# Four reorderings in a two-layer graph-attention kernel: a PSUM copy changes engine, two casts, the score product and a transpose change place

## What is computed

```python
q, k, v = heads(x @ Wq + bq), heads(x @ Wk + bk), heads(x @ Wv + bv)       # 6 heads of 64
probs = softmax(q @ k.T / 8 + where(adj, 0, -9e15))
x = layernorm(x + concat(probs @ v) @ Wf + bf)
h = einsum('bnd,ade->bane', x, W); th = tanh(h)                              # 12 heads of 32
attn = leaky_relu(th @ w_src + (th @ w_dst).T, 0.2); attn = where(adj, attn, -999)
f = elu(softmax(attn) @ h + b); gate = sigmoid(x @ H_w.T + H_b)
x = layernorm(x + gate * f + (1 - gate) * x)
```

## Time and profile before

| | before |
|---|---|
| median of 3 runs | 1189.36 us (1188.29 to 1189.74) |
| the profiled execution, its own time | 1188.84 us |
| its span in the profile | 1187.0 us |
| TensorE busy | 1109.9 us, 94% |
| VectorE busy | 954.3 us, 80% |
| ScalarE busy | 945.2 us, 80% |
| GpSimd busy | 543.9 us, 46% |
| mean granted TensorE clock | 0.988 of full speed |

### The profile page before, as it was taken

The page is one execution under the profiler, slowest core; times in us unless marked ns, Lnnn a source line. Parts: engine busy times, 40 slices in busy tenths (PEclk is TensorE's granted clock), DMA queues, the critical chain, the costliest instruction groups (busy, mean ns, idle before and its releaser), DMA issues.

```text
span 1187.0 us, 25718 instructions
## 1 busy us (share of the span) xinstructions
PE 1109.9 (94%) x8428; PEld 902.9 (76%) x8428; DVE 954.3 (80%) x1958; ACT 945.2 (80%) x3447; POOL 543.9 (46%) x717
## 2 busy tenths in 40 slices
PE   6889999999999999999999999999999999997873
PEld 5667887878787787878778788877878877786652
DVE  5457888888888888888888887888888788888875
ACT  3248888888888888888888888888888888878875
POOL 0454544364454435445444544544454454444332
PEclk9899999999999999999999999999999999999997
DMA  9101001020100101010010101002010100100000
GB/s 257 54 2 54 15 25 57 8 68 15 61 15 18 65 8 68 15 60 15 15 63 12 68 15 61 15 8 68 14 68 15 62 15 8 41 15 15 15 14 21
DMA packets 25894, 44.67 MB, mean 38 GB/s; under 512 B 2462, under 2 KB 23714, under 8 KB 25762
## 3 DMA queue, kind: packets, MB, share of 16 engines
q1 hardware_dynamic: 23234, 41.91, 10.4%
q10 hardware_dynamic: 2496, 1.12, 0.5%
q0 software_dynamic: 32, 0.00, 0.0%
HBM read 30.43 MB, written 12.58 MB: 36 GB/s over the span
## 4 chain that ended last, share of the span: by engine, by line
PE 59%; ACT 23%; issue 8%; POOL 5%; DVE 3%; DMA 1%; ACTq 0%; POOLq 0%; DVEq 0%
ACT z L588 15%; PE ps_b L255 15%; PE ps_a L255 12%; PE ps_d L255 9%; PE ps_s L364 4%; ACT p1T L598 3%; PE ps_s L356 3%; PE ps_c L474 3%; POOL xT_lo L921 3%; PE ps_d L464 3%; PE ps_d L452 3%; PE ps_d L448 3%; PE ps_c L482 2%; ACT gate L664 2%; PE ps_b L411 1%
## 5 line engine op out<-in xcount | busy, mean ns | idle before, releaser
L588 ACT ACTIVATE z<-z,s 128x128 f32<-128x128 f32 x768 | 298.8, 402 | 0.5 <-DVE s L798 0.5
L958 POOL TENSOR_SCALAR s<-s 128x1 f32<-128x1 f32 x128 | 28.6, 224 | 311.8 <-DVE s L892 287.2
L973 POOL TENSOR_TENSOR p<-p,s 128x768 f32<-128x768 f32 x64 | 94.3, 1473 | 147.3 <-DVE s L804 147.3
L615 ACT ACTIVATE p<-ps_s,s 128x128 f32<-128x128 f32 x384 | 135.5, 372 | 29.4 <-DVE s L776 29.0
L588 ACT ACTIVATION_READ_ACCUMULATOR z<-z,s 128x1 f32 x768 | 154.4, 201 | 0.0
L464 PE MATMUL ps_d<-ident,z 128*128 128x128 f32 x768 | 120.0, 279 | 18.4 <-ACT z L588 8.9
L908 DVE SCALAR_TENSOR_TENSOR z<-ps_d,z 128x512 f32<-128x512 f32 x192 | 119.2, 676 | 6.3 <-ACT z L685 6.3
L981 POOL TENSOR_TENSOR thw<-th,w_sd 128x768 f32<-128x768 f32 x64 | 117.7, 1839 | 8.7 <-ACT th L636 8.5
L464 PEld LDWEIGHTS ps_d<-ident,z 128*128 128x128 f32 x768 | 90.7, 141 | 33.0 <-ACT gate L664 18.2
L598 ACT ACTIVATE p1T<-ps_d 128x512 f32<-128x512 f32 x192 | 113.4, 591 | 0.7 <-PE ps_d L464 0.7
L921 POOL TENSOR_TENSOR xT_lo<-x_cols,xT_hi 128x768 fp32r<-128x768 f32 x30 | 54.0, 1821 | 112.8 <-ACT xT_hi L555 112.8
(11 more groups left out here) (157 smaller groups left out, 3536.1 us busy)
## 6 DMA issues: line engine op xcount, KB each, us to landing
x_cols<-in_xT_dram SPq DMA_DIRECT2D x16, 768.0 KB, 6.4
xb<-in_x_dram SPq DMA_DIRECT2D x16, 768.0 KB, 4.9
out_dram<-y SPq DMA_DIRECT2D x64, 192.0 KB, 1.8
z<-in_L_gnn_Wq_dram SPq DMA_DIRECT2D x1, 576.0 KB, 6.3
p1T<-in_L_gnn_Wk_dram SPq DMA_DIRECT2D x1, 576.0 KB, 8.2
qT<-in_L_gnn_Wv_dram SPq DMA_DIRECT2D x1, 576.0 KB, 10.6
kT<-in_L_gnn_Wf_dram SPq DMA_DIRECT2D x1, 576.0 KB, 12.8
z<-in_L_gnn_W_dram SPq DMA_DIRECT2D x1, 576.0 KB, 11.6
```

The lines of the kernel that those rows point to most:

```text
L588: done = act.activation(z[:, a, :], z[:, a, :], ACT.Exp, bias=neg1[:, a:a + 1], accum_out=sum1[:, a:a + 1])
L615: last = act.activation(p0[:, o, i, :], ps_s[:, o, i * N:(i + 1) * N], ACT.Exp, bias=neg0[:, k:k + 1], accum_out=sum0[:, k:k + 1])
L973: pool.tensor_tensor(p0[:].rearrange("p o i n -> p (o i) n"), p0[:].rearrange("p o i n -> p (o i) n"), inv0.unsqueeze(2).broadcast_to([P, ...
```

## The change

It touches three engines' orders. TensorE: the mask and the scores of batch ta+1 are issued right behind `context` of batch ta (before: the mask behind `logits`, the scores at the head of the next turn), and `turn_f` stands behind `fill_a`. VectorE: the maximum of the scores of ta+1 stands behind `cols_R`; the reciprocal and scaling of f stand behind the second maxima; the first copy of p1T is made here, between the split and `cols_R`. ScalarE: that copy is gone, and the two casts of x in j = 3 stand behind the first and behind the second copy of v.

```diff
 # TensorE
-                        scores(g, 1 - par, j)
-                    if has_tail(n, j, 2):
-                        turn_f(tl - 2)
+                            scores(0)
                     if gat:
                         turn_x1(tl, place(j, LAG, par), att)
                     if qkv:
                         fill_a(g, n, j)
+                    if has_tail(n, j, 2):
+                        turn_f(tl - 2)
...
                         context(ta, g, 1 - par, j, n)
+                    if 0 <= ta and ta + 1 < B:
+                        scores_mask(ta + 1)
+                        scores(ta + 1)
                     if gat:
                         project_gate((1,))
...
                         logits(tl)
-                    if 0 <= ta and ta + 1 < B:
-                        scores_mask(ta + 1)
 # ScalarE
                         evacuate_v(0)
+                    if qkv and n + 1 < NG and j == 3:
+                        x_hi(g + 1, 0)
...
                         evacuate_v(2)
+                    if qkv and n + 1 < NG and j == 3:
+                        x_hi(g + 1, 1)
...
-                    if tail:
-                        turned_p1(tl - 1, 0)
...
-                    if qkv and n + 1 < NG and j == 3:
-                        x_hi(g + 1, 0)
-                        x_hi(g + 1, 1)
 # VectorE
+                def turned_p1(t, q):
+                    dve.wait_ge(S["p1_turned"], 3 * t + q + 1)
+                    if due(t):
+                        dve.wait_ge(S["ph_made"], t)
+                    dve.tensor_copy(p1T[:, 4 * q:4 * q + 4, :], ps_d[:, q, :].rearrange("p (a n) -> p a n", a=4)
+                                    ).then_inc(S[f"p1T_{q}"], 1)
...
                         lo_part(x1T, ps_b, slice(0, N), "x1_hi", tl + 1, "x1_lo")
+                    # evacuate_v(1), neg1[0:8], inv0, neg1[8:12] now stand here, ahead of:
                     if has_tail(n, j, 2):
                         # reciprocal of sum1, ps_f scaled in place
...
+                    if tail:
+                        turned_p1(tt, 0)
                     if gat:
                         dve.wait_ge(S["sd_turned"], tl + 1)
                         # cols_R
+                    if 0 <= ta and ta + 1 < B:
+                        scores_maximum(ta + 1)
                     if has_tail(n, j, 2):
                         # r1 and its statistics
```

More of the change, by code:

```diff
@@ L347, in scores_mask, with scores @@
                               mask[:, t, :].unsqueeze(1).broadcast_to([P, C, N]), start=True, stop=False)
-            def scores(g, par, j):
+            def scores(t):
+                par, j = t // G % 2, t % G
                 if j == 0:
-                    pe.wait_ge(S["qk_a_ready"], 3 * g)
-                    pe.wait_ge(S["qk_b_ready"], 3 * g)
+                    pe.wait_ge(S["qk_a_ready"], 3 * (t // G + 1))
+                    pe.wait_ge(S["qk_b_ready"], 3 * (t // G + 1))
                 for i in range(C):
@@ L765, in evacuate_v, with scores_maximum @@
                     dve.tensor_copy(v[:, par, j, :], ps_b[:, 0:D]).then_inc(S["v_odd"], 1)
+                def scores_maximum(t):
+                    dve.wait_ge(S["scores_ready"], t + 1)
+                    if due(t):
+                        dve.wait_ge(S["exp0_ready"], t)
+                    dve.tensor_reduce(neg0.rearrange("p (o i) -> p o i", o=2),
+                                      ps_s[:, :, 0:C * N].rearrange("p o (i n) -> p o i n", i=C),
+                                      AX_X, ALU.max, negate=True).then_inc(S["neg_ready"], 1)
                 for j in range(G):
@@ L770, in iteration @@
                     gat, tail = has_gat(n, j), has_tail(n, j)
[L771 to L778, removed]
+                    if ta == 0:
+                        scores_maximum(0)
                     if gat:
                         lo_part(x1T, ps_b, slice(0, N), "x1_hi", tl + 1, "x1_lo")
[L781 to L790, removed]
                     if qkv and j == 3:
@@ L807, in iteration @@
                                           ).then_inc(S["neg1_ready"], 1)
+                    if has_tail(n, j, 2):
+                        t2 = tl - 2
+                        dve.wait_ge(S["exp1_ready"], 3 * (t2 + 1))
+                        dve.reciprocal(inv1, sum1).then_inc(S["inv1_ready"], 1)
+                        dve.wait_ge(S["inv1_ready"], t2 + 1)
+                        dve.wait_ge(S["f_turned"], t2 + 1)
+                        dve.tensor_tensor(ps_f, ps_f,
+                                          inv1.unsqueeze(2).broadcast_to([P, H1, D1]), ALU.mult
+                                          ).then_inc(S["f_ready"], 1)
                     if has_tail(n, j, 2):
```

## The result

The changed kernel takes 1251.53 us in the median of 4 runs (1249.47 to 1255.51), beside 1188.82 us for the kernel before on the same chip: a ratio of 1.0531, 95% interval 1.0499 to 1.0563. The forecast was slower, 1243 us, range 1220 to 1256. The profiled execution takes 1249.47 us with a span of 1247.7.

What follows compares the result with a forecast made beforehand. TensorE sets the pace (busy 68.2 of 69.5 us), but the scores enter a VectorE-TensorE loop with 0.64 us of slack. Terms +23.2, +29.3 less 0.7, -4.1, +6.0, +1 on 1188.84 gave 1243 us, range 1220 to 1256.

Steps and rivals of the forecast that it cites:

- The loop with 0.64 us of slack: `turn_sd`, VectorE to x1T_lo, `project_h`, back to `turn_sd`: 15.92 us against a 16.56 turn; scores and mask move inside.
- The loop without ScalarE: Rival, 15%: only the VectorE and TensorE loop remains, turns of 17.10 us, 20.01 in j = 3, total 1221 us.
- the detour over ScalarE: From x1T_lo's end (L) through f's scaling, `fe` and four exponentials: `turn_p1` at L + 5.18, TensorE waiting 0.29 us.
- the forecast turn of 17.39: Turn in j = 0, 1, 2 and n = 16: 6.76 + 5.18 + 4.16 + 1.29 us.
- VectorE's stretch, 6.76: VectorE's unbroken work from `cols_R` to x1T_lo's low part, said to go from 6.87 to 6.76 us with the moved maximum.
- The price of the scores, 1.29: TensorE time that masks (0.42) and scores (0.87) add between `project_h` and `turn_sd`; bounds 1.1 to 1.43 us.
- j = 3: Turn with the second cast ahead of the p0T copy: `context` at L + 9.07, turn 20.74 us against 18.65.
- What costs nothing: VectorE's p1T copy (0.7 us) covered by its pause before `cols_R`; `turn_x1`'s residual wait (some 0.5 us) hidden.
- The sum: Turn differences over all groups added to the profiled 1188.84 us: together +54.7, so 1243.5, given as 1243 us.
- The term of n = 16: Last group, without filling: four turns of 17.39 us against 15.88, adding +6.0 us.
- The clock: Granted clock still 1.00 was a sign of being right; TensorE's pauses lowering it a sign of being wrong.
- the rival in which TensorE stays the bound: Rival, 5%: the wait for `x1_lo` never binds, turns of 16.37 us, total 1163 us, 26 less.

Runs made afterwards that it cites:

- run 1: Kernel before with the scores move alone (mask and scores behind `context`, VectorE's maximum behind `cols_R`): 1263.17 us, ratio 1.0596.
- run 8: Changed kernel with mask and scores moved from behind `context` to behind `turn_sd`, VectorE's maximum behind the tail's statistics: 1188.23 us, ratio 0.998.
- run 4: Changed kernel with f's move alone undone (`turn_f` ahead of `turn_x1`, VectorE scales f ahead of the maxima): 1230.51 us, ratio 1.0332.
- run 6: Changed kernel with the second cast of x behind the p0T copy instead of ahead of it: 1241.6 us, ratio 1.0434.
- run 7: Changed kernel with the first copy of p1T back on ScalarE: 1252.52 us, ratio 1.0522.
- run 3: Changed kernel with VectorE's maximum of the scores back between z and x1T_lo, TensorE's order as changed: 1287.86 us, ratio 1.082.
- run 5: Kernel before with f's move alone (`turn_f` later, f's scaling behind the second maxima): 1219.43 us, ratio 1.0242.
- run 11: Kernel before with the first p1T copy on VectorE and both casts of x moved, the second behind the p0T copy: 1162.38 us, ratio 0.9778.
- run 12: Kernel before with the first p1T copy on VectorE and only the first cast moved, the second left behind the last p1T copy: 1156.63 us, ratio 0.9726.
- run 10: Kernel before with the casts of x alone, at the places of the change: 1172.16 us, ratio 0.9847.
- run 9: Kernel before with the first copy of p1T on VectorE alone: 1172.91 us, ratio 0.9846.

## Why the prediction was right, and where it was off

**The loop with 0.64 us of slack.** Right, and decisive. The scores alone make turns of 17.36 (run 1), and the same matmuls outside the loop 16.38 (run 8). The loop without ScalarE was forecast at 17.10 and measured at 17.35 (run 4); the detour over ScalarE was forecast at 0.29 more and measured at 0.16. So the 0.12 us by which the forecast turn of 17.39 is short is what is left of two errors that partly cancel.

**VectorE's stretch, 6.76.** It is 653.00 - 646.11 = 6.89. I had let the maximum overlap its neighbours by 0.09 at each side. The rows show pauses of 0.03 there: it starts at 647.10 behind a `cols_R` that ends at 647.07, and its follower starts at 648.09 behind its end at 648.06. So moving the maximum shortened nothing. (The terms it entered with, 0.95 - 2 x 0.09 - 0.03, also make 0.74 and not 0.75.)

**The price of the scores, 1.29.** 659.93 - 659.50 = 0.43 and 660.79 - 659.93 = 0.86: right. The bound of 0.1 for a change of shape had been read between `turn_sd` and its follower, where the shape does not change; it comes near what the last section finds, 0.09. But `project_h` to the first `turn_p1` was forecast as 4.84 and takes 658.10 - 653.05 = 5.05, of which 0.12 is a wait. The rest stands at the first matmul of `project_h`: 0.28 us to the next start (653.33 - 653.05), where the kernel before has 0.17. Two things changed there, the wait and `turn_f` just ahead, and either is enough: run 4 has the wait alone and shows 0.28, run 8 has `turn_f` alone and shows 0.26.

**The detour over ScalarE, 5.18.** The exponentials end at 657.85 + 0.20 = 658.05, `turn_p1` starts at L + 5.10. Right, though TensorE waits only 0.12 us there instead of 0.29, being later itself. `turn_p1` to `turn_sd`: 5.53, forecast 5.45. Together 6.89 + 5.10 + 5.53 = 17.52, forecast 17.39.

**j = 3.** `context` at 679.65 is L + 9.13 (L is 670.52), forecast L + 9.07. The turn is 20.95, forecast 20.74. The price of the cast ahead of p0T is measured by run 6 and by the group that has no cast (20.28): 0.67 us, forecast 0.73.

**What costs nothing.** The copy of p1T: right (run 7), with 0.34 us of cover forecast at least and 1.35 found. The wait of `turn_x1` for the residual: 0.58 us, forecast 0.5, and hidden as the forecast said (run 3 takes it away and gains nothing). The waits for xT_lo and the gate are gone in the steady part, as forecast.

**The sum.** With the turns measured: 28 x (17.51 - 16.57) = +26.3, 13 x (20.95 - 18.69) + (20.28 - 18.69) = +31.0, 14 x (17.51 - 17.68) = -2.4, n = 16 +5.6, the first j = 3 +1.4, the start -0.6. Together +61, and the spans differ by 60.7. The forecast +54.7 had the terms +23.2, +28.6, -4.1, +6.0, +1. Of the 6 us missing, 3.1 are in j = 1 and 2, 2.4 in j = 3 and 1.7 in j = 0: the 0.12 us a turn, 0.21 in j = 3, that VectorE's stretch and the start of `project_h` took.

**The term of n = 16** came out (+5.6 for +6.0) by luck. Its turns take 17.51, 17.62, 17.82 and 16.20 us. The last one has no scores in it, since no batch follows, and is 1.2 us shorter than the 17.39 forecast for all four; the prediction overlooked that. In the other three the granted clock fell, and two of them are longer than the steady turn.

**The clock.** One sign of being wrong did come. The prediction named a clock that stays at 1.00 as a sign of being right, and pauses that lower it as a sign of being wrong. It is 1.00 in the steady turns, but in three turns of n = 16 it did fall. They cost little there: at most 0.4 us over the steady turn for the three.

**What the prediction missed** did not harm its number. It costed f's move as one detour of 0.29 us, given the scores early. Its own price is another: 0.40 us a turn and 30 us in all (run 5), by a loop through the first layer's exponentials that the early maximum cuts. It also gave the rival in which TensorE stays the bound too little thought in one way: two of the four parts, the copy and the casts, do fill its holes. Without the other two they are worth 27 us (run 11), and 33 with the second cast left where it was (run 12).

## What to carry to other kernels

Before moving work on the fullest engine to a place that is neutral for that engine, look for the loops that pass through it: add up from the moment another engine is released to the moment it releases back, and compare with the turn. The slack of that loop, here 0.64 us of 16.57, and not the engine's busy share, says what may be put inside. Where a wait goes away and the time stays or rises, as with the largest wait of TensorE in run 3, the wait was slack of a shorter loop, and the parts of a change should be timed one by one: here the copy and the casts gained 27 us, and the scores and f lost 79 on top (1241.6 of run 6 beside 1162.4 of run 11, which have the casts at the same places).

## What the runs showed of the hardware

One more change of the array's shape per turn: runs 8 and 12 have TensorE as the bound with the same matmuls in j = 0 to 2, but run 8 goes to the 64-row shape of the scores and back at a place of its own: six changes of shape a turn instead of five. Its turn is 16.38 against 16.24, 0.14 us more. Across a change of shape both traces show a start distance of 0.20 us (from `apply_p1` to the next group, for one) where two 128-column fp32 matmuls of one shape are 0.11 apart, and in run 8 the last matmul of `logits` is 0.31 ahead of `apply_p1` where two of `logits` are 0.22 apart. So my estimate is 0.09 us for a change, and the rest of the 0.14 belongs to groups that have other neighbours, as `turn_f`. That agrees with the Trainium skill (TensorEngine Tiling (Array Packing), Key Properties), which says that a change of mode drains the engine, and gives no time for it.

The granted clock fell in places where the kernel before kept it. In n = 16 each turn of the changed kernel has one pause of TensorE of 2.17 us, and right behind the first one the windows view (columns as in the earlier trace rows) shows a drop between two levels, 1.00 being 2.4 GHz:

```profile
1118.00:1132.00 14.00, 11.19 (x103) 8.56 (x103) 11.83 (x26) 12.24 (x48) 4.48 (x9) 1.00 0.04 15
1132.00:1137.00 5.00, 4.66 (x19) 3.83 (x20) 4.25 (x9) 2.66 (x11) 3.40 (x3) 0.66 0.01 2
```

It fell behind the second and the third such pause too, and not behind the fourth:

```profile
1184.00:1189.00 5.00, 3.26 (x18) 2.62 (x18) 4.28 (x9) 2.62 (x13) 3.29 (x4) 1.00 0.12 43
```

Four turns of the kernel before in the same stage, with pauses of 1.28 and 1.72 us in each, stayed at full clock, with TensorE busy 80% of the time:

```profile
1066.00:1130.00 64.00, 51.50 (x444) 39.67 (x444) 55.98 (x119) 55.07 (x211) 26.42 (x40) 1.00 0.04 14
```

In run 1 it happened in the steady part as well, behind a pause of 1.65 us in j = 0 (0.89 on average from 540 to 555 us). All 14 groups have that pause, and the clock fell in four of them, n = 8 to 11. A clock that falls in some turns only is a likely source of the 6 us between the fastest and the slowest run of the changed kernel, whose mean granted clocks are 0.984 and 0.976. What tips it these runs do not settle.

The start is in step with the clock as well. The first `turn_sd` comes at 76.5 us in one run and at 83.5 in another, though the kernels differ little ahead of it. The granted clock over the first 84 us is 1.00 in runs 10 and 11 (76.5 and 76.7 us), 0.94 to 0.96 in nine kernels (79.0 to 79.7), 0.92 in run 9 (82.8) and 0.90 in runs 1 and 8 (83.2 and 83.5). Why it fell more in some is open. The windows of run 10 and of run 8:

```profile
0.00:84.00 84.00, 63.06 (x345) 50.20 (x346) 39.72 (x66) 29.65 (x85) 31.49 (x37) 1.00 0.38 110
...
0.00:84.00 84.00, 61.42 (x301) 48.23 (x302) 35.03 (x57) 24.44 (x65) 27.91 (x32) 0.90 0.38 110
```

So a few us between two totals can come from the first 84 us alone, and the distances between `turn_sd` are the safer measure of an order of instructions.
